# Flamingo block on one core: probs@V in two visits a batch, values made once, keys stored six steps ahead

## What is computed

```python
# x (16, 224, 512), ctx (16, 750, 512); 16 heads of 32; all fp32
q = (layernorm(x) @ Wq.T) / sqrt(32);  k = ctx @ Wk.T;  v = ctx @ Wv.T
o = sigmoid(q k^T per head) @ v                      # (16, 224, 512)
x = x + tanh(g_xattn) * (o @ Wo.T)
# tokens of layernorm(x) in order: 8 experts of 448 tokens, 512 -> 2048 -> 512
x = x + tanh(g_ffn) * (gelu(tokens @ w1[e] + b1[e]) @ w2[e] + b2[e])
```

## Time and profile before

| | |
|---|---|
| median of 3 executions | 1721.55 us (1721.13 to 1721.71) |
| the profiled execution's own time | 1722.54 us |
| its span in the trace | 1720.9 us |
| PE busy | 1693.3 us, 98% |
| ACT, DVE, POOL busy | 45%, 40%, 12% |
| DMA | 315.75 MB, 183 GB/s over the span |

### The profile page before, as it was taken

The page is one execution under the profiler, slowest core; times in us unless marked ns, Lnnn a source line. Parts: engine busy times, 40 slices in busy tenths (PEclk is TensorE's granted clock), DMA queues, the critical chain, the costliest instruction groups (busy, mean ns, idle before and its releaser), DMA issues.

```text
span 1720.9 us, 34127 instructions
## 1 busy us (share of the span) xinstructions
PE 1693.3 (98%) x12442; PEld 1497.4 (87%) x12442; DVE 689.6 (40%) x1171; ACT 774.7 (45%) x1007; POOL 210.3 (12%) x303
## 2 busy tenths in 40 slices
PE   6999999999999999999999999899999999999999
PEld 5888888888888888888888888799999999999998
DVE  5323313323314224233233133455556464555554
ACT  5545545445445445455455465334333333333332
POOL 1212212112112112122122121000000000000000
PEclk9999999999999999999999999999999999999999
DMA  8767777777677678677677777445362535435251
GB/s 260 219 185 216 205 203 208 205 204 211 197 204 212 190 213 214 185 221 212 196 211 204 201 205 213 136 141 180 99 214 101 194 122 173 149 121 178 101 182 57
DMA packets 199674, 315.75 MB, mean 183 GB/s; under 512 B 25368, under 2 KB 152672, under 8 KB 199520
## 3 DMA queue, kind: packets, MB, share of 16 engines
q1 hardware_dynamic: 176176, 236.05, 48.4%
q0 software_dynamic: 23344, 77.68, 13.1%
HBM read 235.06 MB, written 78.58 MB: 182 GB/s over the span
## 4 chain that ended last, share of the span: by engine, by line
PE 94%; DMA 3%; DVE 1%; issue 1%; SPq 1%; ACT 0%; POOLq 0%; DVEq 0%; ACTq 0%
PE fill_ps L539 39%; PE scores_ps L704 18%; PE fill_ps L685 13%; PE scores_ps L571 9%; PE heads_ps L585 8%; PE heads_ps L685 5%; DMA k_scr<-k_stage 1%; PE fill_ps L644 1%; DMA ctx_raw<-ctxT_in 0%; DMA probs<-WKT_in 0%; PE scores_ps L539 0%; SPq L312 0%; DMA xnT<-stat_scr 0%; SPq L321 0%; ACT probs L742 0%
## 5 line engine op out<-in xcount | busy, mean ns | idle before, releaser
L742 ACT ACTIVATE probs<-scores_ps 125x1792 f32<-125x1792 f32 x192 | 320.2, 1668 | 97.8 <-PE heads_ps L585 54.2
L539 PE MATMUL fill_ps<-ctx_hl,wK 128*128 128x250 f32 x2304 | 310.1, 284 | 9.5 <-DVE wK L901 8.8
L704 PE MATMUL scores_ps<-ctx_hl,wK 128*128 128x448 f32 x1536 | 316.7, 362 | 0.4 <-ACT st_row L771 0.4
L539 PEld LDWEIGHTS fill_ps<-ctx_hl,wK 128*128 128x128 f32 x2304 | 284.1, 190 | 32.2 <-issue 28.9
L704 PEld LDWEIGHTS scores_ps<-ctx_hl,wK 128*128 128x128 f32 x1536 | 288.0, 188 | 20.5 <-issue 0.8
L539 PE MATMUL fill_ps<-wV,ctx_hl 128*125 128x512 f32 x1152 | 286.3, 398 | 0.0
L539 PEld LDWEIGHTS fill_ps<-wV,ctx_hl 128*125 128x125 f32 x1152 | 208.5, 186 | 49.7
L685 PE MATMUL fill_ps<-wQ,wV 128*128 128x448 f32 x1152 | 243.0, 365 | 0.0
L498 POOL DMA_DIRECT2D k_scr<-k_stage x192 | 139.4, 726 | 767.6 <-DVE k_stage L982 689.4
L685 PEld LDWEIGHTS fill_ps<-wQ,wV 128*128 128x128 f32 x1152 | 216.0, 188 | 16.9
L571 PE MATMUL scores_ps<-q_st,k_st 96*125 96x224 f32 x1536 | 202.5, 274 | 9.8 <-DMA q_st<-q_scr 4.1
(11 more groups left out here) (82 smaller groups left out, 1329.6 us busy)
## 6 DMA issues: line engine op xcount, KB each, us to landing
k_st<-k_scr SPq DMA_DIRECT2D x576, 125.0 KB, 3.1
v_sb<-w_in SPq DMA_DIRECT2D x96, 512.0 KB, 4.6
k_scr<-k_stage POOLq DMA_DIRECT2D x192, 250.0 KB, 3.6
ctx_raw<-ctxT_in SPq DMA_DIRECT2D x48, 500.0 KB, 5.1
q_st<-q_scr SPq DMA_DIRECT2D x192, 112.0 KB, 3.3
k_stage<-w_in SPq DMA_DIRECT2D x32, 512.0 KB, 3.6
q_scr<-q_stage POOLq DMA_DIRECT2D x64, 224.0 KB, 3.8
x_ln<-x_in SPq DMA_DIRECT2D x16, 448.0 KB, 4.6
```

Source lines behind the costliest of these rows:

```text
L539: last = pe.matmul(out_, lhsT(kt, a), rhs(kt, c), start=(kt == 0 and t == 0), stop=(kt == KT - 1 and t == 2))
L704: last = pe.matmul(y_ps[:, dt, 0:T], w2[:, slot, a, k, dt * P:(dt + 1) * P], hid_hl[:, slot, d, k, :], start=(c == 0 and k == 0 and t == 0 ...
L742: nc.scalar.activation(probs[0:ST, s % 3], scores_ps[0:ST, :, 0:2 * L], ACT.Sigmoid, scale=SCALE).then_inc(s_probs, 1)
```

## The change

- `heads` handles two tiles of heads in one visit: 2 visits a batch, at step 6 and at step 0 of the next batch. `probs` grows from 3 to 6 slots, `heads_ps` holds 448 columns, and `o_hi` and `o_lo` take 448 columns at once. Each of the six thirds of a visit has a wait of its own on its sigmoid.
- Values of a batch are made in its own steps 1 to 5, in one copy of `v_sb`. Queries of the next batch are made in steps 7 to 11.
- Keys are made 6 steps ahead in place of 4 and go to a DRAM ring of 6. `k_stage` has 3 slots in place of 4; ACT's copy of a key tile waits until the tile three before it is stored.
- SP gathers the key tile of step s + 3 in step s.
- b = -1 makes six key tiles and two query tiles (before: four, two, and two value tiles). All 8 raw weight halves lie in `probs`; the splits of WV and WO come at steps 4 and 6.
- x, its transpose and x1's transpose share buffers (`x_res`, `x_raw`), with waits for that. In batch 15 the first expert's work is placed anew, and its raw weights lie in other buffers.

The core of the diff:

```diff
+    AHEAD = 6
+    RING = 6
+    VISIT = STEPS // 2
...
-    FILL = [(0, "K", 0), (0, "V", 4), (1, "K", 1), (1, "O", 0), (1, "Q", 2), (2, "K", 2), (2, "O", 1), (2, "V", 5),
-            (3, "K", 3), (4, "K", 4), (4, "Q", 3), (5, "K", 5), (5, "U", 0),
-            (5, "U", 1), (6, "K", 6), (7, "K", 7), (7, "Q", 0), (7, "V", 0), (7, "S", 0), (8, "K", 8), (8, "V", 1), (9, "K", 9),
-            (10, "K", 10), (10, "Q", 1), (10, "V", 2), (11, "K", 11), (11, "V", 3)]
-    OWN = [("K", i) for i in range(8)] + [("V", 4), ("V", 5), ("Q", 2)]
-    FILL_FIRST = [(0, "K", 8), (1, "K", 11), (2, "T", 0), (2, "T", 1), (3, "Q", 0), (4, "Q", 1), (5, "V", 0), (6, "V", 1),
-                  (7, "K", 9), (8, "K", 10)]
-
-
-    FILL_0 = [f for f in FILL if f[1] in "KQVS" and f[1:] not in (("V", 4), ("V", 5))]
-    FILL_0 += [(0, "V", 6), (1, "V", 7), (1, "S", 1), (2, "V", 4), (2, "V", 5)]
-    FILL_LAST = [f for f in FILL if f[1] == "O" or f[1:] in OWN]
-    FILL_LAST += [(2, "Q", 3), (4, "U", 0), (5, "U", 1), (9, "S", 0)]
-    FILL_0.sort(key=lambda f: f[0])
-    FILL_LAST.sort(key=lambda f: f[0])
-    K_FIRST = {8: 1, 11: 2, 9: 3, 10: 4}
+    FILL = [(0, "K", 0), (1, "K", 1), (1, "O", 0), (1, "V", 0), (2, "K", 2), (2, "O", 1), (2, "V", 1),
+            (3, "K", 3), (3, "V", 2), (3, "U", 0), (3, "U", 1), (4, "K", 4), (4, "V", 3), (4, "V", 4),
+            (5, "K", 5), (5, "V", 5), (7, "K", 6), (7, "Q", 0), (8, "K", 7), (8, "Q", 1),
+            (9, "K", 8), (9, "K", 9), (9, "S", 0), (10, "K", 10), (10, "Q", 2), (11, "K", 11), (11, "Q", 3)]
+    FILL_FIRST = [(0, "K", 6), (1, "K", 9), (2, "T", 0), (2, "T", 1), (3, "Q", 0), (4, "Q", 1), (5, "K", 7), (6, "K", 10),
+                  (7, "K", 8), (8, "K", 11)]
+    FILL_0 = sorted([f for f in FILL if f[1] in "KVQS"] + [(0, "Q", 6), (0, "Q", 7), (1, "S", 1)], key=lambda f: f[0])
+    FILL_LAST = [(0, "K", 0), (0, "K", 1), (1, "K", 2), (1, "O", 0), (1, "V", 0), (2, "K", 3), (2, "O", 1), (2, "V", 1),
+                 (3, "K", 4), (3, "V", 2), (3, "K", 5), (4, "V", 3), (4, "V", 4), (5, "V", 5), (8, "U", 0), (8, "U", 1),
+                 (10, "S", 0)]
...
-    W_HI = {2: (4,), 3: (5,), 7: (6,), 8: (7,)}
-    W_LO = {1: (2,), 2: (3, 4), 3: (5,), 7: (6,), 8: (7,)}
-    CTX_HI = {5: 2}
-    CTX_LO = {4: 1, 5: 2}
-    CTX_SPLITS = {6: 0, 7: 1, 8: 2}
-    HIDDEN_AT = {8: (0, 0), 10: (0, 1), 11: (1, 0)}
+    W_HI = {4: (4, 5), 6: (6, 7)}
+    W_LO = {1: (2,), 2: (3,), 4: (4, 5), 6: (6, 7)}
+    CTX_HI = {2: 2}
+    CTX_LO = {2: 1, 3: 2}
+    CTX_SPLITS = {4: 0, 5: 1, 6: 2}
+    HIDDEN_AT = {7: (0, 0), 9: (0, 1), 11: (1, 0)}
...
-        return {"K": b + (i + 4) // STEPS, "V": b + (i < 4), "Q": b + (i < 2), "T": b + 1}.get(kind, b - 1)
+        return {"K": b + (i + AHEAD) // STEPS, "V": b, "Q": b + (i < KT), "T": b + 1}.get(kind, b - 1)
...
-        k_stage = sb("k_stage", [P, 4, 2, SC], F32R)
+        k_stage = sb("k_stage", [P, 3, 2, SC], F32R)
...
-        v_sb = sb("v_sb", [P, 2, 6, D])
-        probs = sb("probs", [P, 3, HEADS, 2 * L])
-        x_ln = sb("x_ln", [P, 2, D])
-        x_t = sb("x_t", [P, KT, L])
+        v_sb = sb("v_sb", [P, 6, D])
+        probs = sb("probs", [P, VISIT, HEADS, 2 * L])
+        x_raw = sb("x_raw", [P, 2 * D])
         x_mr = sb("x_mr", [P, 2, L])
         x_res = sb("x_res", [LT, 2, D])
         x1 = x_res
+
+
+        x_t = x_raw[:, 0:KT * L].rearrange("p (t l) -> p t l", t=KT)
+        x1T = x_t
...
-        w_raw = [probs_flat[:, r * HALF:(r + 1) * HALF] for r in range(5)]
-        w_raw += [v_flat[1][:, r * HALF:(r + 1) * HALF] for r in range(3)]
+        v_flat = v_sb[:].rearrange("p t d -> p (t d)")
+        w_raw = [probs_flat[:, r * HALF:(r + 1) * HALF] for r in range(2 * len(w))]
...
+        def raw_of(e, m, c):
+            if known(e, 0) and m == 1 and c < 2:
+                return x_raw[:, 0:HALF] if c == 0 else k_stage[:].rearrange("p r h s -> p (r h s)")[:, 0:HALF].bitcast(F32)
+            if m == 1:
+                return v_flat[:, c % 2 * HALF:(c % 2 + 1) * HALF]
+            return v_flat[:, 2 * HALF:3 * HALF] if c % 2 == 0 else probs_flat[:, 2 * SLOT:2 * SLOT + HALF]
...
+            def gather_k(n, j):
+                r = j % 4
+                alone(sp, s_k_st[j % RING], 16 * (2 * n + j // RING + 1))
+                alone(sp, s_scores, STEPS * n + j - 3)
...
+                    if s + 3 < STEPS and attends(b):
+                        gather_k(b, s + 3)
+                    if s + 3 >= STEPS and prepares(b):
+                        gather_k(b + 1, s + 3 - STEPS)
+                    if attends(b) and s in (0, 3, 6):
+                        gather_q(b, s // 3 + 1)
+                    if prepares(b) and s == 10:
+                        gather_q(b + 1, 0)
+                    if known(b, B - 1) and s == 0:
                         expert_start()
...
-                        load_ctx(b + 1, nh, npar, {1: 0, 2: 1, 7: 2}[s])
-                    if s == 8 and attends(b):
+                        load_w1(0, 1)
+                    if attends(b) and prepares(b) and s in (1, 2, 5):
+                        load_ctx(b + 1, nh, npar, {1: 0, 2: 1, 5: 2}[s])
+                    if known(b, -1) and s == 4:
+
+                        alone(sp, full["T"], 2)
+                        load_x(x_res[:], 1, s_x_in)
+                    if s == 4 and attends(b) and prepares(b, 2):
 
                         alone(sp, full["U"], 2 * b)
                         alone(sp, s_bn[1], 2 * b)
+                        alone(sp, s_bn[0], 2 * (b + 2))
+                        load_x(x_res[:], b + 2, s_x_in)
+                    if s == (9 if known(b, B - 1) else 7) and attends(b):
+
+                        alone(sp, full["U"], 2 * b)
+                        alone(sp, s_bn[1], 2 * b)
+                        if prepares(b, 2):
+                            alone(sp, s_bn[0], 2 * (b + 3))
                         load_x(x_res[:], b, s_xr_in)
...
+                    if s == 11 and attends(b) and prepares(b, 2):
+                        load_xT(b + 2)
+
+            def load_xT(n):
+
+                alone(sp, s_x_lo, n - 1)
+                alone(sp, s_x1T_st, 16 * (n - 2))
+                sp.dma_start(x_t, io["xT"][bass.ds(n, 1)].rearrange("a p t l -> p (a t) l")).then_inc(s_xT_in, 16)
+                alone(sp, s_stat_st, 16 * n)
...
+                if known(e, 0) and c == 0:
+                    alone(sp, s_x_lo, B - 1)
+                    alone(sp, s_x1T_st, 16 * (B - 2))
+                if known(e, 0) and c == 1:
+                    for r in range(RING):
+                        alone(sp, s_k_st[r], 16 * 2 * B)
+                if known(e, 0) and c > 1:
+                    alone(sp, s_av, STEPS * B)
...
             def expert_start():
 
-                alone(sp, s_av, STEPS * (B - 1))
-                load_w2(0, 0)
+                load_xt(0)
+                load_norm(0)
                 load_w1(0, 0)
-                load_w1(0, 1)
-                load_xt(0)
                 load_b1(0)
...
-            def heads(b, par, mt):
-
-                if mt == 0:
+            def heads(b, h):
+
+                if h == 0:
...
-                            last = pe.matmul(heads_ps[j * HD:(j + 1) * HD, 0:L],
-                                             v_sb[0:ST, par, 2 * pair + t, mt * P + j * HD:mt * P + (j + 1) * HD],
-                                             probs[0:ST, pair, j, t * L:(t + 1) * L],
-                                             start=(pair == 0 and t == 0), stop=(pair == 2 and t == 1))
-                    last.then_inc(s_av, 1)
+                at(pe, s_o_lo, 2 * b + h)
+                for mt in (2 * h, 2 * h + 1):
+                    cols = slice(mt % 2 * L, (mt % 2 + 1) * L)
+                    for pair in range(3):
+                        step = 3 * mt + pair
+                        pe.wait_ge(s_probs, STEPS * b + step + 1)
+                        for t in range(2):
+                            for j in range(HEADS):
+                                last = pe.matmul(heads_ps[j * HD:(j + 1) * HD, cols],
+                                                 v_sb[0:ST, 2 * pair + t, mt * P + j * HD:mt * P + (j + 1) * HD],
+                                                 probs[0:ST, step % VISIT, j, t * L:(t + 1) * L],
+                                                 start=(pair == 0 and t == 0), stop=(pair == 2 and t == 1))
+                        last.then_inc(s_av, 1)
...
-                        heads(b - 1, 1 - par, KT - 1)
-                    if s > 0 and s % 3 == 0 and attends(b):
-                        heads(b, par, s // 3 - 1)
+                        heads(b - 1, 1)
+                    if s == VISIT and attends(b):
+                        heads(b, 0)
...
-                at(act, s_av, STEPS * b + s - 2)
-                if known(b, 0) and s == 0:
-
-                    act.wait_ge(s_w_lo, IN_PROBS)
-                nc.scalar.activation(probs[0:ST, s % 3], scores_ps[0:ST, :, 0:2 * L], ACT.Sigmoid,
```

(43 more changed lines are left out.)

262 lines of the change are left out of this document (111 added, 151 removed).

## The result

The changed kernel takes 1771.6 us in the median (1770.7 to 1776.5) against 1721.6 for the kernel before: ratio 1.030, interval 1.027 to 1.032. That is 50 us slower, where 1724.4 was forecast and the range ended at 1733. The span of its profiled execution is 1769.0 us, 48.1 more than before.

The account below looks back on a forecast made before the run. PE was taken as the bound, through its own instruction costs and stalls. Span 1720.9 - 10.2 (visits) + 0.5 (middle) + 13.8 (start) - 1.2 (batch 15) = 1723.8 us, median 1724.4, range 1716 to 1733.

Parts of the forecast that it names:

- What bounds the kernel: Whole kernel: PE busy 1693.3 of 1720.9 us; only its instructions' start-to-start costs or its stalls can move the end.
- Visits: Attention batches: 32 of 64 visit entries and exits go, 0.32 us each, 10.2 us gained (bounds 6.1 and 10.6).
- The six waits inside a visit: Inside each new visit: waits cost nothing while PE's queue runs ahead; if that cover failed, 14 us.
- Middle batches: Steps 7 to 11 of middle batches: no stall expected, thin cover; 0.5 us lost over all batches, between 0 and 8.
- rival 2: Steps 7 to 11: late stores hold ACT's `k_stage` slot, or shifted buffers slow matmuls; 7.5 us more, 1731.9; chance 17%.
- The start: Before batch 0's second scores: ACT's key copies wait for stores, holding up queries and first sigmoid; 13.8 us lost.
- PE's side behind the query gather: At the start: Q0's gather behind K7 lands at about 43 us; scores and three fills behind it end at 50.
- Batch 15 and behind it: Last batch and after: query-gather stall goes, smaller new gaps come; net gain 1.2 us, between 5 gained and 4 lost.
- the third rival: Batch 15: new gaps of 1 to 2 us lower PE's clock, 2.3 us more, 1726.7; chance 11%.
- S's wait of 0.4 us: Behind the last visit: S waits some 0.4 us longer, part of 1.4 us lost there.
- the cheap start: Rival at the start: stores land in 2 to 3 us or full clock comes sooner; 1716 to 1718 us; chance 17%.

Follow-up runs that it names:

- the cut visit: Kernel with query gather first and new first list, its step-0 visit cut in two around a key fill in 15 batches: 1727.4 us, ratio 1.004.
- the list mended alone: Changed kernel with only the fill list before the first batch reordered (K, T, T, Q, Q, then the other keys): 1765.0 us, ratio 1.025.
- the gather moved alone: Changed kernel with the next batch's first query gather moved ahead of the key gather at step 10: 1738.3 us, ratio 1.008.
- with both: Changed kernel with the query gather moved ahead at step 10 and the first fill list reordered: 1723.8 us, ratio 1.001.
- the kernel with batch 0 mended: Kernel with query gather first, new first list and no loop; batch 0's normalising and split of next x one step earlier: 1705.0 us, ratio 0.990.

## Why the prediction was wrong

**What bounds the kernel** was right: PE, and only PE's own costs or its stalls could move the end.

**Visits**: right. Forecast 0.32 us for each removed entry and exit, measured 0.10 + 0.09 + 0.14 = 0.33, some 10.6 us in all, and seen again in the cut visit. The six waits inside a visit cost nothing, as forecast. What the visits do not explain: a batch without a gap is 1.00 us shorter than before (65.51 in place of 66.51), and two visits fewer are 0.66 of it. Another 0.19 is a value fill behind the visit at step 0 that took 2.99 us in the kernel before, where others take 2.80; the rest is spread in hundredths. The prediction had no term for these 0.34 us a batch, and by luck they hid some 5 us of the middle's loss.

**Middle batches**: this step failed. It said of SP's queue that "each gather is asked for four steps before its use, as before, so the loads of x and of the context that it is moved past have 10 us of room". That holds for key gathers, whose wait is for the scores four steps before. The query gather was not looked at: it is asked for at step 10, two steps before its use, and it stands behind the gather of key tile 1, which waits for a store of step 8. By the prediction's own durations the store is issued 1.7 us behind a fill that ends 5.9 us behind the start of step 7, lands 3.6 later at 11.2, the key gather takes 1.3 us to issue and the query gather as long, and lands 3.3 us later: 17.1, against 18.3 when PE wants it. The margin was 1.2 us, and it had to be counted. Then the landings came later than the median taken: 4.7 us for a store in place of 3.6, 4.2 us for a query gather in place of 3.3, with 249 GB/s in steps 8 to 11 and 158 in steps 1 to 3. At the old landings the gather in the batch shown would have landed near 662, just in time for 662.3; so the place used up the room and the crowd turned it into a gap. (The prediction counted 5.8 MB for steps 7 to 11; in their 18.3 us the trace has 200 GB/s, 3.7 MB, rising to 263 GB/s from 655 us on.) The crowding was named (rival 2), but its way was put through ACT's wait for a slot of `k_stage`, which never held ACT in the middle batches: its last wait for a key store is the one at 45.58 us.

The price of the middle, 0.5 us in all with 8 as the most, was too low for two more reasons. First, the clock: in or behind 7 of the 14 gaps it fell to the level of 1.2 GHz, which cost 1.7 to 3.2 us each, so that the gap of 2.20 us above cost 4. Second, the loop's jumps, at which the prediction had no term at all, though a stall of 0.74 us stood there in the trace of before. Against 14 batches of 65.51 us these 14 take 48.9 us more: 30.2 of idle time before first scores (1.5 before), about 16 at the low clock, the rest in small sums; the kernel before had 2.6 over its 66.51. With 14 x 1.00 gained, 48.9 - 2.6 - 14.0 is the 32.3 of the table. Some 10 of it are the two jumps with their low clock, more than in the kernel before.

The trace of before had the warning in plain sight: the one large stall of its batches, 4.10 us, was a query gather stuck in SP's queue, and the prediction told that as a thing that the change would cure.

**Batch 0**: no term either. Its query fill at 90.09 us waits 3.46 us for DVE's subtraction, with the low clock behind it; mended, this gave 4.1 us.

**The start**: right in mechanism and size, 14.1 us against 13.8. Queries at 25.03 us (24.2 forecast), second scores at 50.25 (49.8 to 50.0). What it said in passing, that PE's side behind the query gather ends at the same time, turned out to matter: with the list mended alone 6.7 us came back, with the gather moved alone nothing at the start, with both 14.4.

**Batch 15 and behind it**: right. At equal work the stretch gained 2.1 us, 1.8 forecast. Gaps on PE's timeline of the changed kernel:

```profile
1123.20 2.74 PE L707 MATMUL fill_ps<-wQ,wV 128*128 128x448 f32 x12 [1.79 <-DVE wV L1078]
...
1128.66 1.10 PE L592 MATMUL scores_ps<-q_st,k_st 96*125 96x224 f32 x8 [1.08 <-ACT probs L764]
...
1134.98 1.10 PE L592 MATMUL scores_ps<-q_st,k_st 96*125 96x224 f32 x8 [1.75 <-ACT probs L764]
...
1146.17 5.79 PE L560 MATMUL scores_ps<-wO,oT 128*112 128x512 f32 x24 [1.40 <-DVE oT L991]
...
1155.61 5.13 PE L707 MATMUL fill_ps<-wQ,wV 128*128 128x448 f32 x24 [0.44 <-DVE wV L1078]
```

1.79, 1.08 and 1.75 us were forecast as 2.1, 1.2 and 1.8; 1.40 behind the last visit as 1.4; 0.44 as 0.6. The low clock behind the third gap was not in the forecast: `hidden` behind it takes 4.10 us in place of 2.44, so the third rival, the clock in batch 15, was true for one of its four gaps, at 1.7 us. Smaller gaps than forecast made up for it, and S's wait of 0.4 us, forecast as new, was in the kernel before too (0.42 us). That the sum came out so close is in part luck.

**The other rivals**: the cheap start did not happen; the first store landed 6.2 us after its issue at 15.66. Crowding (rival 2) came, by another path and at several times the price that it named.

## What to carry to other kernels

For every item that an in-order queue holds, write down when it is issued and when its user wants it, counting the waits of everything ahead of it in that queue; a margin "for the gathers" is worth nothing if one kind of gather has another lead. Repeated gaps of 1 to 4 us on PE are to be priced above their length, here at about one and a half times in sum and at double for some, since the clock can go with them. And when the order of a loop's body is changed, compare the matmul time that PE has queued at the jump back with how long its branch takes in the trace.

## What the hardware showed

- Behind gaps of 1.75, 2.20 and 2.55 us PE's granted clock fell to the level of 1.2 GHz (at 1136, 665 and 177 us of the changed kernel), while it stayed at full speed behind others of 1.48 and 2.04 us. The length of the gap alone doesn't tell which it will be: a gap of 1.75 us did it and one of 2.04 us did not, and the same gap of 1.79 us in batch 15 was followed by full speed in the changed kernel (`hidden` 2.58 us) and by the lower level in the kernel with batch 0 mended (3.77 us).
- At a loop's jump back PE's compare-and-branch took 3.84 and 3.86 us in the kernel before and 3.97 to 7.86 us in the others, while those of ACT, DVE, POOL and SP took 0.04 to 0.07 us. PE's gap is what is left of it when the queued matmuls are done: 0.74 us with 3.52 us of matmuls queued, 2.3 to 6.2 us with 2.07.
- At the same bytes a batch, moving the requests together raised the median landing of a key store from 3.6 to 4.7 us; with one load of 448 KB moved out of steps 7 to 9 it was 4.1.
